# A two-layer graph attention kernel: source scores of the last blocks from W2 folded with the source vector, score rows sent through DRAM, and W1 loaded head by head

## The reference

```python
def _gat_layer(x, src, dst, W, a_src, a_dst, bias, concat):
    h = (x @ W).reshape(N, H, C)
    al_s = einsum('nhc,hc->nh', h, a_src)
    al_d = einsum('nhc,hc->nh', h, a_dst)
    e = leaky_relu(al_s[src] + al_d[dst], 0.2)
    m = segment_max(e, dst)
    ex = exp(e - m[dst])
    alpha = ex / (segment_sum(ex, dst)[dst] + 1e-16)
    out = segment_sum(h[src] * alpha[:, :, None], dst)
    return (concat or mean over heads of out) + bias

h = elu(_gat_layer(x, ..., W1, att_src1, att_dst1, b1, concat=True))    # 768 -> 4 heads x 512
o = _gat_layer(h, ..., W2, att_src2, att_dst2, b2, concat=False)        # 2048 -> 768, one head
out = layernorm(x + o)
```

## Time and profile before

| what | value |
|---|---|
| median of 3 runs | 938.28 us (937.78 to 938.47) |
| the profiled execution | 937.02 us, its span 935.1 us |
| TensorE matmul busy | 881.1 us (94%) |
| VectorE busy | 602.1 us (64%) |
| ScalarE (ACT) busy | 424.4 us (45%) |
| GpSimd (POOL) busy | 198.1 us (21%) |
| moved by DMA | 111.18 MB |
| start to the first window | 0 to 38 us |
| count windows, scores, first h | 38 to 185 us |
| first layer | 185 to 602 us |
| second product | 602 to 799 us |
| second layer and norm | 799 to 935 us |

### The profile page before, as it was taken

One profiled execution on the slowest core, in us unless ns is written; L12 is line 12 of the kernel. 1 busy time (PEld: TensorE's weight loads), 2 busy tenths in 40 slices (PEclk: granted clock), 3 DMA queues, 4 the chain that ended last, 5 costly groups with the idle time before them and its releaser, 6 DMA issues.

```text
span 935.1 us, 15156 instructions
## 1 busy us (share of the span) xinstructions
PE 881.1 (94%) x5719; PEld 796.9 (85%) x5719; DVE 602.1 (64%) x1169; ACT 424.4 (45%) x686; POOL 198.1 (21%) x134
## 2 busy tenths in 40 slices
PE   4998879999999999999999999989999999699996
PEld 2455557799888998889988899989999999599996
DVE  9458663668873889638895488672223334497886
ACT  5456452276643866339652396661111111487300
POOL 1000000144212332124321244300000000155452
PEclk9999989999999999999999999999999999799999
DMA  8609999462548237472174243655223322400223
GB/s 298 145 14 132 178 174 159 135 211 81 177 138 239 67 103 212 112 231 78 29 214 139 68 142 117 174 166 115 72 48 70 85 48 30 102 1 2 69 84 95
DMA packets 64450, 111.18 MB, mean 119 GB/s; under 512 B 31772, under 2 KB 33464, under 8 KB 63004
## 3 DMA queue, kind: packets, MB, share of 16 engines
q1 hardware_dynamic: 64379, 110.22, 45.7%
HBM read 85.25 MB, written 24.94 MB: 118 GB/s over the span
## 4 chain that ended last, share of the span: by engine, by line
PE 67%; DVE 11%; issue 9%; POOL 6%; ACT 3%; DMA 2%; DVEq 1%; SPq 1%; POOLq 0%; ACTq 0%
PE ps L1726 19%; PE ps L1728 19%; PE ps L1727 19%; POOL pbuf L608 5%; PE ps L1755 3%; PE ps L1696 2%; PE ps L1847 2%; PE ps L1686 1%; DVE pbuf L621 1%; DVE h2f L1632 1%; DMA mask_scratch<-nbs 1%; DVE h2f L1606 1%; DVE vbuf L1440 1%; DMA w1f<-in_L_gnn_W 1%; DVE bnst L1623 1%
## 5 line engine op out<-in xcount | busy, mean ns | idle before, releaser
L608 POOL TENSOR_TENSOR pbuf<-pbuf,grow 125x625 f32<-125x625 f32 x100 | 169.9, 1700 | 701.2 <-ACT pbuf L593 261.1
L1726 PE MATMUL ps<-hx,PThi 125*125 125x260 f32 (+5 forms) x800 | 227.3, 284 | 3.0 <-DVE vbuf L1441 2.5
L1728 PE MATMUL ps<-hx,PTlo 125*125 125x260 f32 (+5 forms) x800 | 225.4, 282 | 0.0
L1727 PE MATMUL ps<-hlo,PThi 125*125 125x260 f32 (+4 forms) x800 | 224.9, 281 | 0.0
L1726 PEld LDWEIGHTS ps<-hx,PThi 125*125 125x125 f32 x800 | 148.7, 186 | 7.0 <-DVE vbuf L1441 2.9
L1727 PEld LDWEIGHTS ps<-hlo,PThi 125*125 125x125 f32 x800 | 149.1, 186 | 1.4
L1728 PEld LDWEIGHTS ps<-hx,PTlo 125*125 125x125 f32 x800 | 149.0, 186 | 0.0
L1726 PE MATMUL ps<-W2p,hT 128*125 128x384 f32 x320 | 109.7, 343 | 3.2 <-DVE hT L1453 1.7
L1728 PE MATMUL ps<-W2p,hT 128*125 128x384 f32 x320 | 108.1, 338 | 0.0
L1727 PE MATMUL ps<-W2p,hT 128*125 128x384 f32 x320 | 108.1, 338 | 0.0
L621 DVE SCALAR_TENSOR_TENSOR pbuf<-pbuf,counts 125x625 f32<-125x625 f32 x100 | 90.7, 907 | 25.3 <-ACT pbuf L615 25.2
(11 more groups left out here) (186 smaller groups left out, 1571.6 us busy)
## 6 DMA issues: line engine op xcount, KB each, us to landing
xr<-xT_scratch SPq DMA_DIRECT2D x30, 750.0 KB, 4.9
nbm<-mask_scratch SPq DMA_DIRECT2D x40, 273.4 KB
hidden_scratch<-vbuf SPq DMA_DIRECT2D x40, 224.0 KB
hblk<-hidden_scratch SPq DMA_DIRECT2D x10, 896.0 KB
xT_scratch<-xa SPq DMA_DIRECT2D x20, 375.0 KB, 11.7
w1f<-in_L_gnn_W SPq DMA_DIRECT2D x12, 512.0 KB, 9.1
w1raw<-in_L_gnn_W SPq DMA_DIRECT2D x4, 1536.0 KB, 7.9
w2raw<-in_L_gnn_W SPq DMA_DIRECT2D x14, 384.0 KB, 5.4
```

Source lines behind the costliest of these rows:

```text
L608: pool.tensor_tensor(pslot(c), pslot(c), src[:, g * GN:(g + 1) * GN], ALU.add).then_inc(e_done, 1)
L1726: pe.matmul(dst, ahi, bhi, start=start, stop=False, skip_group_check=shared)
L1727: pe.matmul(dst[:, 0:n], ahi, blo, start=False, stop=False, skip_group_check=shared)
L1728: return pe.matmul(dst, alo, bhi, start=False, stop=stop, skip_group_check=shared)
```

## The change

In the start, W1 comes in eight transfers, two for each head, and the fold steps wait for head 0, head 1, and heads 2 and 3 together. TensorE loads two window plans ahead of the folding; the next two are loaded before windows 8 and 12. VectorE's loads stay.

In the first layer, W2 is loaded once more in sixteen blocks of 128 rows (`wf2`), and VectorE multiplies each with the source vector and sums over the columns (`w2a`), in the second group of heads 0 to 2. The 2048 sums go to DRAM.

Between the layers, the source scores of blocks 8 and 9 are made from the hidden rows `hblk` and the folded vector, which comes back in three parts (`prow`): `late_dots`, `late_scores`. The scores of blocks 7 to 9 go to DRAM and back together. The second and third parts of the maxima stand before block 8's scores. The target scores and the shift go through DRAM in two halves of five blocks (`store_column`, `load_row`) in place of TensorE's spreads. ACT and VectorE prepare the first chunk before `h2_out(9)` and `scores2(9)`. Several buffers change their place.

```diff
+FOLD2 = tuple((h, b) for h in range(H - 1) for b in ((0, 1, 5, 8, 9) if h < H - 2 else (0, 1, 5, 7, 8, 9)))
@@ SP @@
-            for i in range(2):
-                for k in range(KD):
-                    sp.dma_start(w1f[:, 2 * i:2 * i + 2, k, :], W1[k * 128:(k + 1) * 128, 2 * i * HC:(2 * i + 2) * HC]
-                                 .rearrange("p (h c) -> p h c", h=2)).then_inc(ld_wf[i], 16)
+            for h in range(H):
+                for k in range(0, KD, KD // 2):
+                    sp.dma_start(w1f[:, h, k:k + KD // 2, :], W1[k * 128:(k + KD // 2) * 128, h * HC:(h + 1) * HC]
+                                 .rearrange("(k p) c -> p k c", p=128)).then_inc(ld_wf[min(h, 2)], 16)
...
+            def load_fold2(h, b):
+                if (h, b) in FOLD2:
+                    i = FOLD2.index((h, b))
+                    if i > 0:
+                        sp.wait_ge(fold2_done, i)
+                    sp.dma_start(wf2[:], W2[128 * i:128 * i + 128, :]).then_inc(ld_fold2, 16)
...
+            def store_column(to, col, g):
+                for lo, hi in RP:
+                    sp.dma_start(to[g * GT:(g + 1) * GT].rearrange("b p -> p b")[lo:hi, :], col[lo:hi, :],
+                                 allow_slow_non_contiguous=True).then_inc(g_stored, 16)
+            def load_row(row, src, g, landed):
+                for lo, hi in RP:
+                    sp.dma_start(row[lo:hi, g * GN:(g + 1) * GN], spread_row(src.rearrange("b p -> (b p)")[g * GN:(g + 1) * GN], hi - lo)
+                                 ).then_inc(landed, 16)
...
+            load_prow(1)
+            load_prow(2)
+            sp.wait_ge(ht_ps, 2 * NB - 2)
+            load_part(1)
+            sp.wait_ge(al2_done, 2 * NB - 4)
+            sp.wait_ge(s2_late, 1)
+            store_s2(NB - 3, NB)
+            load_part(2)
+            sp.wait_ge(s2_stored, RS * (NB - 2))
+            load_s2(NB - 3, NB, ld_s2[QP])
+            sp.wait_ge(g_stored, RS * H)
+            load_row(drow2, d2_d, 0, ld_drow[0])
+            sp.wait_ge(g_done, H + 1)
+            store_column(g2_d, gcol[:, H * NB:H * NB + GT], 0)
+            sp.wait_ge(g_stored, RS * (H + 1))
+            load_row(grow2, g2_d, 0, ld_grow[0])
@@ ACT @@
+                if b == NB - 2:
+                    act.wait_ge(mx_last, QP * NB)
...
             act_exp(act, CHUNKS)
+            act_hi(act, CHUNKS)
+            act_exp(act, CHUNKS + 1)
+            h2_out(NB - 1)
+            act.wait_ge(h2_sb, NB)
@@ VectorE @@
+                if g == 1 and (h, b) in FOLD2:
+                    i = FOLD2.index((h, b))
+                    dve.wait_ge(ld_fold2, RS + 16 * (i + 1))
+                    dve.wait_ge(fold2_done, i)
+                    dve.scalar_tensor_tensor(wf2junk[:], wf2[:], 1.0, as2row[:], ALU.mult, ALU.mult, accum_out=w2a[:, i:i + 1]).then_inc(fold2_done, 1)
...
                 if b == 7:
                     maxima2(8)
                     maxima2(9)
+                    late_dots(1)
                     for m in range(4):
                         part_maxima2(0, m)
                 if b == 8:
+                    for m in range(NB):
+                        part_maxima2(1, m)
+                    merge(1)
+                    for m in range(6):
+                        part_maxima2(2, m)
+                split_hT(2 * b + 3)
+                if b == 8:
+                    for m in range(6, NB):
+                        part_maxima2(2, m)
+                    merge(2)
+                    shift2(0)
+                scores2(b)
+                if b == 6:
+                    late_dots(0)
+                if b == 7:
+                    late_dots(2)
+                    late_scores()
...
+            split_h2(0)
+            dve_counts(dve, CHUNKS)
+            dve_lo(dve, CHUNKS)
+            scores2(NB - 1)
+            shift2(1)
@@ TensorE @@
-            ahead = [windows_plan(mybir.EngineType.PE, q) for q in range(Q0)]
+            ahead = [windows_plan(mybir.EngineType.PE, q) for q in range(Q0 // 2)]
...
-            spread(lambda n: al2[:, 0, n:n + 1], lambda b: (7, 0), NB - 1, NB).then_inc(bc2_ps, 1)
-            pe.wait_ge(al2_done, 2 * NB)
-            spread(lambda n: al2[:, 1, n:n + 1], four_from(0)).then_inc(bc2_ps, 1)
-            pe.wait_ge(g_done, H + 1)
-            for g in range(2):
-                spread(lambda n: gcol[:, H * NB + n:H * NB + n + 1], lambda n: (4 + n // GT * 2 + n % GT // BB, n % GT % BB * B),
-                       g * GT, (g + 1) * GT).then_inc(bc2_ps, 1)
+            pe.wait_ge(hx_one, 2)
...
+                    if c == 0 and u < 2:
+                        pe.wait_ge(h2_sb, NB - 1 + u)
```

More of the change, by code:

```diff
@@ L317, in gat_kernel @@
         h2lo = sb("h2lo", [B, NB, D], F32R)
-        PT2 = [sb(f"PT2_{i}", [B, 2, GN], F32R) for i in range(3, PR2)] + PT2
+        PT2 = [PT2[2], PT2[1]] + [sb(f"PT2_{i}", [B, 2, GN], F32R) for i in range(3, PR2)] + [PT2[0]]
         assert cursor[0] <= base0 + 2 * KC * D * 4
@@ L330, in gat_kernel @@
         ld_an = sem("ld_an")
-        ld_wf = [sem(f"ld_wf{i}") for i in range(2)]
+        ld_wf = [sem(f"ld_wf{i}") for i in range(3)]
         xT_stored = sem("xT_stored")
@@ L590, in act_relu @@
             src, bias = (drow, s_up[:, h, b:b + 1]) if h < H else (drow2, s2_up[:, b:b + 1])
-            if h < H and b == 0:
+            if b == 0:
                 act.wait_ge(ld_drow[g], RS * (h + 1))
@@ L863, in _ @@
             load_part(0)
-            for b in range(NB - 1):
-                if b + 3 < NB:
-                    load_hb(b + 3)
-                elif b + 3 == NB:
-                    sp.wait_ge(ht_ps, 2 * NB - 2)
-                    load_part(1)
-                else:
-                    sp.wait_ge(ht_ps, 2 * NB)
-                    load_part(2)
-                store_s2(b)
-                load_s2(b)
+            for b in range(NB - 3):
+                load_hb(b + 3)
+                sp.wait_ge(al2_done, 2 * b + 1)
+                store_s2(b, b + 1)
+                sp.wait_ge(s2_stored, RS * (b + 1))
+                load_s2(b, b + 1, ld_s2[max(0, b // 2 - 1)])
                 if b == 4:
@@ L1517, in scores2 @@
                 if b > 0:
-                    dve.wait_ge(al2_done, 2 * b)
-                for v in range(2):
+                    dve.wait_ge(al2_done, 2 * b if b < NB - 1 else 2 * NB - 3)
+                for v in range(2) if b < NB - 2 else (1,):
                     dve.scalar_tensor_tensor(a2junk[:, v, :], h2f[:, b, :], 1.0, a2row[:, v, :], ALU.mult, ALU.mult,
@@ L1553, in merge, with late_dots, late_scores, shift2 @@
                 dve.tensor_tensor(mx[:, lo:hi], mx[:, lo:hi], mxp[:, p * NB:(p + 1) * NB], ALU.max).then_inc(mx_all, 1)
-            for b in range(NB):
-                if b > 0 and b + 1 < NB:
+            dots = bnst[:, 0:2, 0, 0:len(PP)]
+            def late_dots(p):
+                lo, hi = PP[p]
+                dve.wait_ge(ld_a2, 2 * RS + RS * (p + 1))
+                dve.wait_ge(al2_done, 2 * NB - 6 if p < 2 else 2 * NB - 4)
+                for b in (NB - 2, NB - 1):
+                    if p > 0 or b == NB - 1:
+                        dve.wait_ge(dot_done, 2 * p + b - NB + 2)
+                    if p == 0:
+                        dve.wait_ge(ld_hb[b % 2], RS * (b // 2 + 1))
+                    dve.scalar_tensor_tensor(a2junk[:, 0, 0:hi - lo], hblk[:, b % 2, lo:hi], 1.0, prow[:, 0:hi - lo], ALU.mult, ALU.mult,
+                                             accum_out=dots[:, b - NB + 2, p:p + 1]).then_inc(dot_done, 1)
+            def late_scores():
+                dve.wait_ge(dot_done, 2 * len(PP))
+                dve.tensor_reduce(al2[:, 0, NB - 2:NB], dots, AX.X, ALU.add).then_inc(s2_late, 1)
+            def shift2(g):
+                lo, hi = H * NB + g * GT, H * NB + (g + 1) * GT
+                dcol = al2[:, 1, g * GT:(g + 1) * GT]
+                dve.wait_ge(mx_all, QP)
+                dve.wait_ge(al2_done, (2 * GT, 2 * NB - 2)[g])
+                dve.scalar_tensor_tensor(mneg[:, lo:hi], mx[:, lo:hi], -1.0, dcol, ALU.mult, ALU.subtract).then_inc(m_neg, 1)
+                dve.wait_ge(m_neg, H + 1 + g)
+                dve.scalar_tensor_tensor(negm[:, lo:hi], mneg[:, lo:hi], SLOPE, mneg[:, lo:hi], ALU.mult, ALU.min).then_inc(m_sb, 1)
+                dve.wait_ge(m_sb, H + 1 + g)
+                dve.scalar_tensor_tensor(gcol[:, lo:hi], negm[:, lo:hi], 1 / SLOPE, dcol, ALU.mult, ALU.add).then_inc(g_done, 1)
+            for b in range(NB - 1):
+                if b > 0:
                     split_hT(2 * b + 2)
@@ L1569, in _ @@
                     merge(0)
-                if b + 1 < NB:
-                    split_hT(2 * b + 3)
-                if b == NB - 1:
-                    for m in range(NB):
-                        part_maxima2(1, m)
-                    merge(1)
-                scores2(b)
             def split_h2(b):
@@ L1581, in split_h2 @@
```

(8 more changed lines are left out.)

131 lines of the change are left out of this document (73 added, 58 removed).

## The result

The changed kernel takes 941.77 us (median of 20 runs, 938.10 to 944.03), the kernel before 938.17 (20 runs, 933.95 to 940.32): ratio 1.0039, interval 1.0027 to 1.0050. It is 0.4% slower, some 3.7 us. I had forecast 934.7, with 939.5 as the upper end of the range. The profiled execution has a span of 938.5 us against 935.1.

A forecast was written before the change was run, and what follows sets the result against it. The start of the second layer's add, exp, relu loop was taken to bound the end. Start -1.6, first layer 0, between the layers -1.9 sum to -3.5 us: 934.7 us median, own range 931 to 937.5, full range 929.5 to 939.5.

The forecast's parts named there:

- lower bound of -7: Between the layers: net gain of 7 us if both DRAM trips' stores take 6.6 us and rows are short.
- Start, -1.6 forecast: Start: folding 2.6 us earlier, less 0.7 and 0.3 for late plan loads; -1.6 us, bounds -2.6 and +4.2.
- First fold at 13.0: Start: with two plans loaded ahead, TensorE's folding starts at 13.0 us, 2.6 earlier than 15.62.
- the price of window 12: Start: plan load of 2.5 us before window 12, mostly hidden by a VectorE wait and products; costs 0.3 us.
- The start gives nothing: Rival, start: xT and mask stores met at 92 to 102 us set the pace; 936.4 us, chance 0.15.
- First add, 807.2 forecast: Between the layers: first second-layer add can start at 807.2 instead of 810.51, 3.3 us earlier.
- Part 1 of the folded row can be asked for at 757.31 + 0.75 and lands at 762.5: Between the layers: part 1 is requested after block 6's store at its old time, leading to late scores at 771.0.
- the trips take over the bound: Rival, between the layers: store_s2 and store_column with SP's waits; at 10.1 us each, 938.6 us; chance 0.08.
- Loop, +1.4 forecast: Second layer: work moved behind the first add makes the fourth add come 10.3 us after it, not 8.9; +1.4 us.
- The first layer at 0: First layer: VectorE's sixteen dots and SP's sixteen loads are hidden by VectorE's lead; price 0.
- the stall of TensorE that nothing depends on: Between the layers: TensorE gets the split of hT at 791.9, wanted at 790.5; a harmless 1.4 us stall.
- The rule of the Trainium skill: Between the layers: a DMA's fixed cost is about 2.0 us, so the two stores would cost 12 us less.

The follow-up runs named there:

- plans_at8: Changed kernel with both late window plan loads before window 8, instead of one before window 8 and one before 12; 946.43 us, 1.0086 to the kernel before.
- start_only: Kernel before with only the new start (W1 by head in two transfers each, two plans ahead, two later); 937.29 us, 0.9996 to the kernel before.
- target_late: Changed kernel with the store of the first five target columns moved behind the loads of the folded row's parts 1 and 2; 944.27 us, 1.0062 to the kernel before.
- loop_order: Changed kernel with ACT's last eviction ahead of exp 0, VectorE's last score and second shift ahead of counts 0; 943.39 us, 1.0048 to the kernel before.
- target_last: Changed kernel with the first five target columns stored behind the load of the last three blocks' score row; 942.88 us, 1.0029 to the kernel before.
- split_first: Changed kernel with the split of hT(19) ahead of the sixteen partial maxima that wait for the late score row; 944.26 us, 1.0060 to the kernel before.
- probe: Separate kernel without the computation, timing SP's stores and loads: one column 6.6 to 7.8 us, 500-byte row 1.1, 125 rows of 512 bytes 1.7.
- combo_spread: Changed kernel with the four moves, and the shift row's first half spread by TensorE and copied by ACT, not through DRAM; 930.60 us, 0.9916 to the kernel before.
- four moves: Changed kernel with split_first, loop_order, target_last and folded row's part 1 requested before the wait on block 6's store; together 935.64 us, 0.9968 to the kernel before.

## Why the prediction was wrong, step by step

The sum was -3.5 us; the spans differ by +3.4. The miss of 6.9 us has three terms, 1.9 + 4.0 + 1.2, less 0.2 us that the changed kernel gained at the end of the first layer, where I had forecast 0. Two sums of the prediction are off beside that: the walk to the first add gives 807.1, and its lower bound of -7 comes out as -5.7 with stores of 6.6 and rows of 3.8 us.

**Start, -1.6 forecast, +0.3 read (miss 1.9).** First fold at 13.0: right (13.16). Of the 2.5 us, 2.0 are left at window 0 and 0.8 at window 8 (0.7 forecast for its load, 1.2 read). The step that failed is the price of window 12, "0.3 (2.5 - 1.3 - 0.9 of products)": from 0.7 ahead to 1.8 behind it cost 2.6. The load took 3.5 us, not 2.5; 0.9 of it lay under products, and the 1.3 us wait for VectorE behind it was covered, as forecast. What the sum held at nothing is the clock: at 0.87, 0.50 and 0.78 in the three stretches of 2 us from 82 to 88 us, window 12 and its transposes took 3.6 us to window 13, in the kernel before 3.9 with the wait and so 2.6 without it. Some 1.5 us of the loss are made up before the first product. Over all traces P lies between 143.9 and 149.0 us in eleven with the new start, plans_at8 left out (mean 145.8), and at 144.7, 145.0 and 148.6 in three with the old one (mean 146.1). The gaps ahead of P indicate where it is made: plan loads later on, under xT stores, hold TensorE for 0.5 to 3.6 us, and around 130 to 143 it waits 1 to 3.6 us for VectorE's ring. That this ring absorbs what is gained is argued from these rows, not shown by a run. The clock is a rival to it: in four of the eleven (start_only, target_late, loop_order, target_last) it is at 0.50 from 64 to 70 us, around and behind the gap before window 8, and window 9 then begins 5.3 us after window 8 instead of 3.0. P does not follow it alone, since the shortest P (target_last) is among these four. How much the start gives stays open between 0 and my 1.6 us; the times of start_only (1.9 faster to 1.1 slower) hold both. "The start gives nothing" was a rival, at 0.15, with another mechanism.

**First add, 807.2 forecast, 811.2 read (miss 4.0).** The readings are the changed kernel's times less 0.06 us, the distance of TensorE's rows of the two traces between 620 and 780 us. By terms: late scores at 771.0, read 774.1 (+3.1); their store 8.2, read 8.1; their row 3.8, read 5.8 (+2.0); VectorE's block 11.5, read 11.4; the shift's store 8.2, read 6.65 (-1.5); its row 4.4, read 5.2 (+0.8). The step that failed first is "Part 1 of the folded row can be asked for at 757.31 + 0.75 and lands at 762.5". It was asked for at 762.3, 4.2 us later, and its dot began at 765.6, 3.1 us later, which is the whole delay of the late scores. Of the 4.2 us 1.7 are block 6's store and its wait, and 2.5 the issue of the row's load behind it. I had taken the old times of both, though the change puts part 0 of the folded row and 625 single elements into the queue ahead of them, and ahead of block 9's rows that the dots need. Taking those elements away brought the store from 13.1 to 7.2 and 7.75. The rows of the load times were taken from a quieter queue as well. The rival "the trips take over the bound" named the place, and held that only slower stores could bring the other side; the two stores it spoke of took 14.7 us together, less than my 16.4. What carried the time up lay in front of the first of them and behind both, in a store I had not counted and in rows.

**Loop, +1.4 forecast, +2.6 read (miss 1.2).** From the first add to the last reciprocal it is 119.55 us, before 116.91. The mechanism was right, and loop_order bears it out. The size was off: VectorE's second shift takes 1.14 us for its first operation, the counts of chunk 1 and ACT's high part 1 come behind it in a row, and ACT then waits 1.8 us.

**What held.** The first layer at 0, but for the 0.2 us; the stall of TensorE that nothing depends on (6.3 us instead of 1.4; without it, in split_first, E fell by about the split's own length); no price per column in a store; VectorE's block between the trips. The rule of the Trainium skill that I had set against my rows (DMA: Bandwidth & Descriptors, Anatomy of one DMA: about 2.0 us fixed) is given there for DMAs that GpSimd issues; these are SyncE's. It is near the probe's stores of contiguous rows, 1.1 and 1.7 us, and far from the single elements, 6.6 to 8.9 us; by the measurement, not by the rule, a trip of a column is dear.

**Where the expected gain went.** The shift was to be 13.3 us earlier; it is 8.4 earlier (799.3 against 807.76). The trip that follows takes 11.9 us from that shift to the first add, the spread it replaced 2.8. So the change gains 8.4 us on the scores and pays 9.1 on the shift, and the first add comes 0.7 us later. combo_spread keeps the one and takes back the other: 8 us faster than the kernel before.

What stays open: why a column of single elements takes 7 us when 512-byte rows take 1.7, and why block 6's store took 10.9 us in the first trace and 12.8 to 14.5 in the five of later jobs that had the same transfers ahead of it. The request for part 1 behind it differs less, 14.1 us after the store's issue against 14.4 to 15.3, since the issue of the row's load took 3.2 us in the first trace and 0.7 to 1.5 in the five.

## What to carry to other kernels

When a change puts a DMA into a queue, cost again every transfer and wait behind it, even those that the diff doesn't touch: the old trace's time for them is no longer theirs. Make a round trip through DRAM where its result has slack (the late scores, the targets) and keep on-chip spreads for a value that the next stage waits for. Where an early gain is to reach the end, look for the next engine that the path has to wait for, and measure the parts together as well as one by one; here four moves gave 5 to 6 us singly and 8.0 together by single traces, and 11.6 and 10.5 by the times.

## What the hardware showed that I had not expected

- A store of single 4-byte elements from 125 partitions takes 6.6 to 7.8 us in empty queues, five times as many 8.5 to 8.9, ten times 8.4 to 8.5; one 500-byte row takes 1.1. Two such stores in a row take about the sum of both, 15.7 and 14.9 us, though the queues move next to nothing.
- TensorE's granted clock was 0.57 on the mean from 793 to 801 us, around and behind a standstill of 6.3 us, and 1.00 in the same stretch of split_first, where TensorE did not pause; E moved by no more than its scatter.
- TensorE pauses for 1.47 us, until 2 to 3 us before window 8, in every trace, and for another 0.7 to 1.0 us before window 8 with the new start. In four of eleven such traces the granted clock is 0.50 from 64 to 70 us, in the other seven 1.00, and window 8 took 5.3 us instead of 3.0.
- P, made of the same instructions, swings by 5 us between traces of kernels with the same start, and the changed kernel's loss was 0.39% in the first timing and 0.80% in a later job.
